# A fused transformer block: the down product truncated on ScalarE through integer writes, and the second attention's loop in another order

## The reference

```python
x = x + tanh(g_xattn[0]) * L0_xattn(layernorm(x), ctx)      # 32 heads, 8 kv heads, q and k normalised
x = x + tanh(g_ffn[0])   * L0_ffn(layernorm(x))             # gate and up to 1376, integer intermediate
x = x + tanh(g_xattn[1]) * L1_xattn(ctx, ctx, layernorm(x)) # 128 x 128 similarity per row, softmax
x = x + tanh(g_ffn[1])   * L1_ffn(layernorm(x))             # router, top 2 of 16 experts, 2 shared parts
```

```python
inter_q = trunc(clip(inter * 128.0, -128.0, 127.0)).astype(int8)
down = einsum('bsi,hi->bsh', inter_q.astype(float32), w_down)
out = trunc(clip(down * 128.0, -128.0, 127.0)).astype(int8)
```

## Time and profile before

| what | value |
|---|---|
| median of 3 runs | 1288.28 us (1287.07 to 1289.25) |
| the profiled execution's own time | 1284.16 us |
| its span, first to last instruction | 1282.2 us |
| mean granted TensorE clock | 0.976 of full |
| TensorE / VectorE / ScalarE / GpSimd busy | 94% / 64% / 45% / 28% |
| chain that ended last, by engine | PE 54%, DVE 24%, issue 10%, ACT 6%, POOL 4% |

### The profile page before, as it was taken

How to read it: one execution, slowest core, us unless ns; L and a number is a source line. 1 busy time by engine, 2 the same in 40 slices (tenths; PEclk the granted TensorE clock), 3 DMA queues, 4 the chain that set the end, 5 groups by cost and what they waited for, 6 DMA issues and landing times.

```text
span 1282.2 us, 20367 instructions
## 1 busy us (share of the span) xinstructions
PE 1199.4 (94%) x6791; PEld 1018.2 (79%) x6791; DVE 818.2 (64%) x2400; ACT 575.7 (45%) x1349; POOL 358.4 (28%) x307
## 2 busy tenths in 40 slices
PE   7899999999999999999999999969999888789992
PEld 6788898888988898889888888847877665567771
DVE  6667667667676766676767666766878688531113
ACT  4545555455445554545545545433443323233340
POOL 5413023122121321312302312123333133165551
PEclk8999999999999999999999999989999998899996
DMA  7001001000000100101100000011223227233425
GB/s 262 1 34 50 1 34 50 1 33 16 33 33 0 49 10 23 49 0 33 49 0 33 0 1 1 25 27 53 74 74 94 74 74 265 104 99 127 132 79 197
DMA packets 37447, 73.51 MB, mean 57 GB/s; under 512 B 6098, under 2 KB 22482, under 8 KB 35349
## 3 DMA queue, kind: packets, MB, share of 16 engines
q1 hardware_dynamic: 30708, 56.33, 13.0%
q0 software_dynamic: 4960, 12.33, 3.1%
q10 hardware_dynamic: 1728, 4.20, 0.9%
HBM read 64.45 MB, written 12.32 MB: 60 GB/s over the span
## 4 chain that ended last, share of the span: by engine, by line
PE 54%; DVE 24%; issue 10%; ACT 6%; POOL 4%; DMA 1%; SPq 1%; DVEq 0%; ACTq 0%; POOLq 0%
PE bank L335 13%; PE bank L337 12%; PE bank L336 12%; PE bank L1873 4%; ACT probs L773 3%; DVE iq L1258 3%; DVE probs L1116 2%; PE bank L1621 2%; PE bank L1891 2%; DVE k_junk L1073 2%; PE bank L1757 2%; DVE row_max L1089 2%; DVE pt_lo L1103 1%; POOL k_rstd L556 1%; PE bank L1563 1%
## 5 line engine op out<-in xcount | busy, mean ns | idle before, releaser
L773 ACT ACTIVATE probs<-bank,exp_bias,q_rstd 128x256 f32<-128x256 f32 x256 | 141.2, 562 | 144.8 <-DVE exp_bias L1097 144.8
L1108 DVE TENSOR_TENSOR o_lo<-bank,o_hi 128x512 fp32r<-128x512 f32 x64 | 44.3, 692 | 185.8 <-ACT o_hi L766 185.7
L335 PE MATMUL bank<-wkv_hi,kv_src_lo 128*128 128x256 f32 x512 | 146.3, 286 | 1.7 <-DVE kv_src_lo L1141 1.7
L337 PE MATMUL bank<-wkv_hi,kv_src_hi 128*128 128x256 f32 x512 | 146.1, 285 | 0.0
L336 PE MATMUL bank<-wkv_lo,kv_src_hi 128*128 128x256 f32 x512 | 146.0, 285 | 0.0
L560 POOL TENSOR_TENSOR q_rstd<-q_var,minus_half 128x8 f32<-128x8 f32 x32 | 52.4, 1637 | 302.8 <-DVE q_var L1076 302.8
L762 ACT ACTIVATE pt_hi<-bank 128x512 fp32r<-128x512 f32 x128 | 69.5, 596 | 115.8 <-PE bank L1621 115.8
L335 PE MATMUL bank<-wo_hi,o_lo 128*128 128x512 f32 x256 | 105.4, 412 | 1.0 <-DVE o_lo L1108 1.0
L335 PE MATMUL bank<-wq_hi,kv_src_lo 128*128 128x512 f32 x256 | 103.2, 403 | 0.8 <-POOL wq_lo L545 0.8
L337 PE MATMUL bank<-wo_hi,o_hi 128*128 128x512 f32 x256 | 102.8, 402 | 0.0
L336 PE MATMUL bank<-wo_lo,o_hi 128*128 128x512 f32 x256 | 102.1, 399 | 0.0
(11 more groups left out here) (261 smaller groups left out, 3116.3 us busy)
## 6 DMA issues: line engine op xcount, KB each, us to landing
weights<-r_w SPq DMA_DIRECT2D x16, 768.0 KB, 8.9
wq_raw<-wq SPq DMA_DIRECT2D x8, 1024.0 KB, 4.8
wo_raw<-wo SPq DMA_DIRECT2D x8, 1024.0 KB, 4.8
wkv_raw<-wkv SPq DMA_DIRECT2D x8, 512.0 KB, 3.4
gu_raw<-w_gate SPq DMA_DIRECT2D x10, 256.0 KB, 3.3
gu_raw<-w_up SPq DMA_DIRECT2D x10, 256.0 KB, 3.5
wd_raw<-w_down SPq DMA_DIRECT2D x10, 256.0 KB, 3.8
x_sb<-x SPq DMA_DIRECT2D x4, 512.0 KB, 9.7
```

The costliest lines, as they stand in the source:

```text
L335: eng.matmul(out_ap, a_lo, b_hi, start=start, stop=False)
L337: return eng.matmul(out_ap, a_hi, b_hi, start=False, stop=stop)
L773: act.activation(probs[:, h, :], scores_ps[h // 2][:, (h % 2) * 256:(h % 2) * 256 + 256], ACT.Exp, bias=exp_bias[:, h:h + 1], scale=q_rstd ...
L1108: dve.tensor_tensor(o_lo[:, par, :], o_ps[:, :], o_hi[:, par, :].bitcast(F32), ALU.subtract)\
```

## The change

The whole part of the down product is made on ScalarE alone. `down_whole` takes Relu(256 v - 0.5) and Relu(-256 v - 0.5) from the bank into `twice` (int32, the write rounds), and from these Identity(+-0.5 y -+ 0.25) into `whole` (int8, the write rounds and saturates), one for each sign. VectorE adds both sides to x. VectorE's three rounding instructions and its clip, and GpSimd's product by the sign, are gone. `twice` and `whole` lie where the `tr_` tiles were. The bias constants cost three memsets at the start.

The loop's order is another on all four engines: TensorE takes the down product in pieces of 4, 4 and 3 chunks with the transposes and the similarity between them, transposes the router's rows ahead of the context product, and starts tile 0's first ten chunks before the last chunk's intermediate is there. VectorE and ScalarE do the router's rows and their low part one step later. The splits of the shared experts' weights come one step later, on GpSimd both `inner_low` before both `outer_low`.

```diff
@@ gpsimd
-            pool.wait_ge(consts_ready, 2)
+            for i, bias in enumerate((-0.5, -0.25, 0.25)):
+                pool.memset(cut_bias[:, i:i + 1], bias).then_inc(consts_ready, 1)
+            pool.wait_ge(consts_ready, 5)
...
             for s in range(NB + 2):
-                if s < NB:
-                    down_sign(s)
                 if 0 <= s - 2 < NB:
                     ln_root(s - 2, 1)
-                if s == NB - 1:
-                    inner_low(0)
                 if s < NB:
                     ln_root(2 * NB + s)
-                if s == NB - 1:
-                    outer_low(0)
-                if s == NB:
-                    inner_low(1)
-                if s == NB + 1:
-                    outer_low(1)
+                else:
+                    inner_low(s - NB)
+            for e in range(SHARED):
+                outer_low(e)
@@ scalar
-            def down_magnitude(t):
+            def down_whole(t):
+
                 cols = slice(t % 2 * D, t % 2 * D + D)
                 act.wait_ge(down_done, t + 1)
-                act.wait_ge(iq_ready, INNER + t - 1)
-                act.activation(tr_abs[:, cols], bank[4 + t % 2][:, :], ACT.Abs, scale=128.0).then_inc(sign_ready, 1)
-                act.activation(tr_sign[:, cols], bank[4 + t % 2][:, :], ACT.Sign, scale=-1.0).then_inc(sign_ready, 1)
+                if t < 2:
+                    act.wait_ge(iq_ready, INNER + t - 1)
+                else:
+                    act.wait_ge(x2_ready, 2 * (t - 1))
+                for side, sign in enumerate((1.0, -1.0)):
+                    act.activation(twice[:, side, cols], bank[4 + t % 2][:, :], ACT.Relu, scale=256.0 * sign,
+                                   bias=cut_bias[:, 0:1]).then_inc(down_cut, 1)
+                for side, sign in enumerate((1.0, -1.0)):
+                    act.wait_ge(down_cut, 4 * t + 1 + side)
+                    act.activation(whole[:, side, cols], twice[:, side, cols], ACT.Identity, scale=0.5 * sign,
+                                   bias=cut_bias[:, 1 + side:2 + side]).then_inc(down_cut, 1)
...
-            down_magnitude(0)
-            for s in range(NB + 2):
+            for s in range(NB + 3):
+                if s < NB:
+                    down_whole(s)
                 if 0 <= s - 1 < NB:
                     ln_high(2 * NB + s - 1, q3[:, :, :])
+                if s == NB:
+                    copy_logits(0)
+                if 0 <= s - 3 < NB:
+                    t = s - 3
+                    ln_high(t, xt_hi[:, :, t * P:t * P + P], 1)
+                    act.dma_start(rows_dram[t * P:t * P + P, :], moe_rows[:, t % 2, :]).then_inc(rows_stored[t % 2], 16)
+                if 0 <= s - 1 < NB:
                     act.wait_ge(sim_bias_ready, s)
                     if s >= 2:
                         act.wait_ge(context_done, s - 1)
                     act.activation(sim[:, :], bank[6][:, 0:P], ACT.Exp, bias=sim_bias[:, :], scale=CTX_SCALE,
                                    accum_out=sim_sum[:, :]).then_inc(sim_exp, 1)
-                if s + 1 < NB:
-                    down_magnitude(s + 1)
-                if s == NB:
-                    copy_logits(0)
-                if s == NB + 1:
-                    silu_of(0)
-                if 0 <= s - 2 < NB:
-                    t = s - 2
-                    ln_high(t, xt_hi[:, :, t * P:t * P + P], 1)
-                    act.dma_start(rows_dram[t * P:t * P + P, :], moe_rows[:, t % 2, :]).then_inc(rows_stored[t % 2], 16)
-                if s == NB - 2:
+                if s == NB - 1:
                     act.wait_ge(down_done, NB)
                     expert_high(0)
-                if s == NB - 1:
+                if s == NB:
                     expert_high(1)
+            silu_of(0)
@@ vector
             def down_add(t):
 
-                k, cols = INNER + t, slice(t % 2 * D, t % 2 * D + D)
-                dve.wait_ge(inter_step, k * 4 + 4)
-                dve.tensor_scalar(tr_int[:, cols], tr_int[:, cols], 127.0, -128.0, ALU.min, ALU.max)\
-                   .then_inc(iq_ready, 1)
...
+                for side in range(2):
+                    dve.wait_ge(down_cut, 4 * t + 3 + side)
+                    dve.scalar_tensor_tensor(out=x_sb[:, t, :], in0=whole[:, side, cols], scalar=gate_rows[:, 2:3],
+                                             in1=x_sb[:, t, :], op0=ALU.mult, op1=ALU.add).then_inc(x2_ready, 1)
+                    dve.wait_ge(x2_ready, 2 * t + 1 + side)
                 ln_stats_of(2 * NB + t, t)
...
-            for s in range(NB + 2):
-                if s < NB:
-                    down_whole(s)
+            for s in range(NB + 3):
                 if 0 <= s - 2 < NB:
                     add_context(s - 2)
+                if s < NB:
+                    down_add(s)
                 if 0 <= s - 1 < NB:
                     sim_max_of(s - 1)
-                if 0 <= s - 3 < NB:
-                    router_in_low(s - 3)
+                if 0 <= s - 2 < NB:
+                    ln_rows_of(s - 2, s - 2, 1)
                 if 0 <= s - 1 < NB:
                     sim_norm(s - 1)
                 if s < NB:
-                    down_add(s)
-                if 0 <= s - 2 < NB:
-                    ln_rows_of(s - 2, s - 2, 1)
-                if s < NB:
                     ln_rows_of(2 * NB + s, s)
-
+                if 0 <= s - 3 < NB:
+                    router_in_low(s - 3)
...
             take_logits(0)
-            router_in_low(NB - 1)
@@ tensor
+            pe.wait_ge(iq_ready, INNER - 3)
+            pe.wait_ge(wd_lo_ready, CH)
+            down(0, 0, CH - 1)
             pe.wait_ge(iq_ready, INNER - 1)
-            pe.wait_ge(wd_lo_ready, CH)
-            down(0, 0, CH)
+            down(0, CH - 1, CH)
             down(1, 0, CH)
             for s in range(NB + 2):
+                if s + 1 == NB // 2:
+                    pe.wait_ge(iq_ready, INNER)
+                if 2 <= s + 1 < NB:
+                    down(s + 1, 0, 4)
                 if 0 <= s - 1 < NB:
                     if s >= 3:
                         pe.wait_ge(ln_hi_ready[0], 2 * NB + s - 2)
                     turn_rows(2 * NB + s - 1)
-                if s + 1 == NB // 2:
-                    pe.wait_ge(iq_ready, INNER)
+                if s == NB - 1:
+                    route(0)
                 if 2 <= s + 1 < NB:
-                    down(s + 1, 0, CH // 2)
+                    down(s + 1, 4, 8)
                 if 0 <= s - 1 < NB:
                     similarity(s - 1)
                 if 2 <= s + 1 < NB:
-                    down(s + 1, CH // 2, CH)
-                if s == NB - 1:
-                    route(0)
-                if s == NB:
-                    pe.wait_ge(ln_hi_ready[0], 3 * NB - 1)
-                    inner_part(0, 0)
-                if 0 <= s - 1 < NB:
-                    context(s - 1)
+                    down(s + 1, 8, CH)
+                if s == NB + 1:
+                    pe.wait_ge(ln_hi_ready[0], 3 * NB)
+                    inner_part(0, 1, range(0, 2))
                 if 0 <= s - 2 < NB:
                     if s - 2 >= 2:
                         pe.wait_ge(ln_lo_ready[1], s - 3)
                     turn_rows(s - 2, 1)
+                if 0 <= s - 1 < NB:
+                    context(s - 1)
                 if s == NB:
-                    pe.wait_ge(ln_hi_ready[0], 3 * NB)
-                    inner_part(0, 1)
+                    pe.wait_ge(ln_hi_ready[0], 3 * NB - 1)
+                    inner_part(0, 0)
+            inner_part(0, 1, range(2, KC))
```

More of the change, by code:

```diff
@@ L25 @@
 I32 = mybir.dt.int32
+I8 = mybir.dt.int8
 U32 = mybir.dt.uint32
@@ L70, in build @@
         head_w = sb("head_w", [P, 3])
+        cut_bias = sb("cut_bias", [P, 3])
         ln_stats = [sb(f"ln_stats{i}", [P, NB, 6]) for i in range(2)]
@@ L157, in build @@
         wd_lo = put("wd_lo", [P, CH, D], F32R)
+        tr_at = at[0]
         tr_v = put("tr_v", [P, 2 * D])
@@ L161, in build @@
         tr_int = put("tr_int", [P, 2 * D])
+        tr_end, at[0] = at[0], tr_at
+        twice = put("twice", [P, 2, 2 * D], I32)
+        whole = put("whole", [P, 2, 2 * D], I8)
+        at[0] = tr_end
         stage_at = at[0]
@@ L479, in _ @@
             load_weights(6, 14)
-            sp.wait_ge(x2_ready, NB)
+            sp.wait_ge(x2_ready, 2 * NB)
             load_weights(14, E)
@@ L1265, in _ @@
                 .then_inc(bias_split, 1)
-            def down_whole(t):
-                k, cols = INNER + t, slice(t % 2 * D, t % 2 * D + D)
-                dve.wait_ge(iq_ready, k)
-                dve.wait_ge(sign_ready, k * 2 + 1)
-                dve.tensor_scalar(tr_int[:, cols], tr_abs[:, cols], ROUND, ROUND, ALU.add, ALU.subtract)\
-                   .then_inc(inter_step, 1)
-                dve.wait_ge(inter_step, k * 4 + 1)
-                dve.tensor_tensor(tr_v[:, cols], tr_int[:, cols], tr_abs[:, cols], ALU.subtract).then_inc(inter_step, 1)
```

(34 more changed lines are left out.)

16 lines of the change are left out of this document (6 added, 10 removed).

## The result

The changed kernel's median is 1267.81 us (1267.04 to 1269.92, four runs) beside 1287.67 us for the kernel before on the same chip: 0.985 of its time, 95% interval 0.983 to 0.9871. The profiled execution took 1269.92 us, its span is 1268.1 us.

The account below looks back on a forecast made before the run. The prediction took each step as bound by a chain with TensorE waiting 1.5 us for VectorE. Terms -4.1 - 7.3 - 2.7 - 4.6 + 2.65 = -16.05 took the median 1288.28 to 1272.2 us; range 1267 to 1281 (0.85).

Parts of the forecast that it names:

- The start: Up to tile 0's similarity row maximum: earlier first down matmuls and the 2.60 us TensorE idle removed, -4.1 us.
- M1: Time mark: VectorE's row maximum of the similarity for tile 0, first of eight, M1 to M8; forecast 1019.14 to 1015.0.
- The steady steps: Five loop steps, one 128-token tile each, from M1 to M6: TensorE sets 7.7 against 9.16 us, -7.3 us.
- The prices that no row showed: int32 and int8 conversions taken at fp32 durations (0.60, 0.63, 0.75), upper bound twice that; Relu and Identity table loads taken as nothing.
- M6 to M7: Between the sixth and seventh row maxima, no down tile left for TensorE: VectorE's 7.1 sets it, before 9.78, -2.7 us.
- M7 to M8: Between the seventh and eighth row maxima, no down tile for VectorE: 5.05 against 9.63, -4.6 us.
- M8 to route(1): Last row maximum to router's second half: inner_low on GpSimd blocks VectorE's normalisation twice, 12.5 against 9.85, +2.65 us.
- The base: Starting time for the difference: median 1288.28, 4.1 above the profiled execution's 1284.16, giving 1272.2 us.
- ScalarE as the bound: Rival: ScalarE's four conversions make the kernel slower, break-even some 2.0 us each; at 2.4 us, 1301; chance 0.06.
- The partial gain: Rival: context hand-over, VectorE's queue or slow int8 read holds steps at 8.4 to 8.9 us: 1277 to 1281; chance 0.22.
- more gain: Rival: VectorE beats inner_low at one or both roots, or TensorE's clock holds: 1268 to 1270; chance 0.08.
- The last weights: Rival of no gain: a fixed release downstream, the last weight loads, gives the gain back: 1285 to 1291; chance 0.04.

Follow-up runs that it names:

- the truncation alone: Kernel before with ScalarE's new truncation and two VectorE additions, loops in the old order: 1283.23 us, ratio 0.998.
- the order alone: Changed kernel's loops with the old truncation (VectorE's rounding and clip, GpSimd's product): 1276.88 us, ratio 0.9929.
- the two runs with two chunks less: Changed kernel without down-product chunks for tiles 2 to 7: 8 and 9 (third piece), 1267.27 us; 2 and 5 (first two pieces), 1264.46 us.
- the changed kernel again: The changed kernel, unedited, run once more as the measure for the others: 1268.1 us, ratio 0.9859.
- the run with the late start: Changed kernel with the old wait, for the last chunk's first half, ahead of tile 0's first down matmul: 1269.97 us, ratio 0.9875.
- the two profiles with `inner_low` ahead: Changed kernel with each inner_low on GpSimd before the root it stood behind, run in two groups: 1263.75 and 1264.31 us.
- the constants alone: Kernel before with only the bias tile and its three memsets added, unused: 1286.13 us, ratio 0.9994.

## Why the prediction came out right

Step by step, by the table above:

- **The start**, forecast -4.1: -4.65 (15.54 for 20.19). The reasons hold: the early start is worth 1.7, and the rest goes with the 2.60 us of idle. M1 of the truncation alone (16.87) and of the order alone (19.49) shows what ends the idle: in the main, tile 0's product coming sooner through the new truncation. VectorE's side was ready as forecast.
- **The steady steps**, forecast -7.3: -7.14 (five of 7.74 for 45.82 us). The size was right and the reason half right. "TensorE sets the step: 7.7" names one of two rings of the same length; the other is the hand-over at context. The forecast had both ("both arrive together; the slack is near nothing") and then took the sum as the sole bound. For the time that made no difference; for the next edit it decides, as the two runs with two chunks less show.
- **The prices that no row showed.** The fp32 durations were the right end for the types. The four ScalarE instructions took 0.684 and 0.720 instead of 0.60 and 0.63, 0.35 a step that lies in ScalarE's idle time. VectorE's addition: 0.75 and 0.747. Relu and Identity brought no table load; the section of the Trainium skill that the forecast cites ("ScalarE: Activation LUTs", "Table sets: the hidden batching unit") has both in every set, and the trace agrees: one load of 1.28 us in the loop, as before.
- **M6 to M7**, forecast -2.7 and VectorE as the bound: 7.09 us, -2.69, and no idle time of VectorE ahead of that maximum. **M7 to M8**, -4.6: 4.98 us, -4.65.
- **M8 to route(1)**, forecast +2.65: 12.49 for 9.85, +2.64. Two rows started behind inner_low, 2.39 and 2.62 us. The sum is right, its parts less so. The 0.4 for inner_part at 1.2 GHz was in the wrong place: its matmuls were 0.43 us apart up to 1074.84, but its last one before tile 7's transposes starts at 1077.46 and those at 1077.83, set by the rows, so that cost nothing. The lower clock was paid by tile 6's context product, 1.41 us for 1.02; in the changed kernel again it took 1.76 (M8 to route(1) 12.85), and in the run with the late start 1.92, behind transposes of 1.09 (13.40). Besides, tile 6's rows ended 0.3 us earlier than forecast, and from tile 7's rows to route(1) it took 2.4 us for 2.15. That the order of two GpSimd instructions is the whole of it is shown by the two profiles with `inner_low` ahead: 3.1 to 3.4 us less in the stage (75.63 and 75.68 for 78.78 and 79.07). The Trainium skill, "SBUF — State Buffer", section "SBUF: two separate sides", has the pair of ports that VectorE and GpSimd share as an exclusive lock whose loser is fully blocked. The traces agree: the rows took 2.39 and 2.62 us beside inner_low (2.35 and 2.40), 1.43 beside outer_low, 0.55 alone.
- **The sum**: -16.05 forecast, -16.49 between the stages of the two profiles. **The base** is the term that was mis-sized. I added the 4.1 us by which the median of three runs of before stood above its profiled execution (1284.16). The three later groups put that median at 1286.3 to 1286.9, so 2.2 to 2.8 above it. From 1286.37 the stages' 16.2 to 16.5 lead to some 1270, and the same group's median is 1268.1: about 2 us more were gained. Two profiles that were taken close to the median of their kernels (1286.13 and 1268.1) show where: the constants alone at 1286.27 and the changed kernel again at 1268.19 are 18.08 us apart, and 17.59 of it is the stage (96.66 and 79.07). The profile that the forecast stands on is a quick execution, in which TensorE's low clock missed tile 7's similarity. That is one pair of executions; how often the clock falls there, no run shows. And it is partly luck that the median (1267.81) came where the sum from the profile alone had pointed (1268.1): a start 2.2 us too low and a gain some 2 us too small cancel.
- **The rivals.** ScalarE as the bound would have needed 2.0 us an instruction; it has 0.72. (The rule that the forecast cites there, from the Trainium skill's "ScalarE: Activation LUTs", "Rules for kernel authors", gives VectorE's speed for bf16; these rows are fp32, 0.42 for 0.63 us.) The partial gain would have shown in steps of 8.4 or more; none is above 7.75. The time is next to that of the rival "more gain" (1268 to 1270), but what this needed did not happen: VectorE was never ahead of inner_low in the changed kernel, and TensorE's clock fell. The forecast's "one such row" was one of two: in the trace of before the normalised rows of tile 7 (first_rows, at 1080.03) also took 1.48 us, beside outer_low at 1079.97. The last weights took nothing back: from route(1) to the end it is 187.98 us in both profiles.

## What to carry to other kernels

Before taking work from a busy engine, follow one tile around the loop from one hand-over to the same one in the next step: where that ring is longer than each engine's load, only another order shortens it, and then the same cut pays. When two rings are equally long, a cut outside one of them is worth nothing, so ask of each piece of work which rings it lies in. And a long GpSimd operation right behind the small one that VectorE waits for can cost VectorE nearly its full length (here 2.39 and 2.62 us for an operation of 0.55); put it ahead, where GpSimd is idle. A profile is one execution: before its time is used as a base, see where it stands among the other runs.

## What the runs showed of the hardware

- An activation of 128x512 that writes int32, or reads int32 and writes int8, takes as long as in fp32: 0.684 and 0.720 us. VectorE's fused multiply and add that reads int8 takes 0.747, for 0.752 in fp32.
- Beside inner_low (2.35 to 2.40 us on GpSimd) VectorE's normalised rows took 2.39 or 2.40 us for tile 6 and 2.60 to 2.62 for tile 7, in all six profiles of kernels with the changed kernel's order on GpSimd and its truncation, and ended about 0.3 us after it. GpSimd's next instruction starts 0.07 us before VectorE's that waited for the same root. In the run with the order alone tile 6's rows start 1.56 us into inner_low and take 1.07, again ending 0.3 us after it.
- TensorE's clock differs between executions of one kernel, and where its low stretches fall moves the time. At the end of the loop it accounts for the spread of 12.49, 12.85 and 13.40 us for the same work from M8 to route(1) (above). Another place is the end of the first attention, which no edit touches. From 850 to 866 us, first the changed kernel, then the same one again:
```profile
850.00:866.00 16.00, 10.98 (x49) 9.35 (x48) 12.16 (x24) 6.49 (x16) 2.86 (x2) 0.71 0.00 1
```
```profile
850.00:866.00 16.00, 10.10 (x49) 8.32 (x48) 12.15 (x25) 6.49 (x15) 3.41 (x3) 0.82 0.00 1
```
The granted clock is 0.71 in one and 0.82 in the other, and the stage then begins 2.0 us later (1001.34 and 999.36). At 840 us the two executions are 0.2 us apart. What decides it, no run here shows.
